# Value projection in units of one chunk, with both weight parts in one matmul and the halves added on DVE

## What is computed

```python
k = (cond @ wk.T + bk).reshape(B, L, H, D).transpose(0, 2, 1, 3)
v = (cond @ wv.T + bv).reshape(B, L, H, D).transpose(0, 2, 1, 3)
scores = jnp.einsum('bhnd,bhld->bhnl', q, k) * inv_sqrt_d + mask[:, None]
attn = jax.nn.softmax(scores, axis=-1)
o = jnp.einsum('bhnl,bhld->bhnd', attn, v)
```

## Time and profile before

| | |
|---|---|
| three runs | 997.35, 997.23, 993.93 us (median 997.23) |
| profiled execution | 993.16 us; span of its instructions 991.5 us |
| PE busy | 915.1 us, 92% of the span |
| PE's weight loads busy | 779.1 us, 79% |
| ACT busy | 565.5 us, 57% |
| DVE busy | 559.7 us, 56% |
| TensorE's granted clock, mean | 0.962 |

### The profile page before, as it was taken

One profiled execution on the slowest core, in us unless ns is written; L12 is line 12 of the kernel. 1 busy time (PEld: TensorE's weight loads), 2 busy tenths in 40 slices (PEclk: granted clock), 3 DMA queues, 4 the chain that ended last, 5 costly groups with the idle time before them and its releaser, 6 DMA issues. The chain is left out here.

```text
span 991.5 us, 21367 instructions
## 1 busy us (share of the span) xinstructions
PE 915.1 (92%) x7803; PEld 779.1 (79%) x7803; DVE 559.7 (56%) x1054; ACT 565.5 (57%) x976; POOL 74.5 (8%) x83
## 2 busy tenths in 40 slices
PE   5945989999999999999999999999999999979995
PEld 3534579898888888888888888888888888867773
DVE  2695465546565556565646564656555655563424
ACT  2513166766565656565756666666666666663442
POOL 0021000000000000000000000000000000063453
PEclk8965699999999999999999999999999999999998
DMA  6009657575656666656675666566656676420001
GB/s 177 7 34 258 155 130 166 130 161 143 149 146 146 155 137 151 146 151 135 157 150 145 138 157 147 152 136 160 146 153 137 158 149 141 98 46 2 2 0 38
DMA packets 67814, 126.19 MB, mean 127 GB/s; under 512 B 23568, under 2 KB 52408, under 8 KB 67512
## 3 DMA queue, kind: packets, MB, share of 16 engines
q1 hardware_dynamic: 66384, 124.66, 52.8%
q10 hardware_dynamic: 1344, 0.23, 0.2%
HBM read 46.30 MB, written 4.65 MB: 51 GB/s over the span
## 5 line engine op out<-in xcount | busy, mean ns | idle before, releaser
L1248 ACT ACTIVATE probsT<-ps_T 125x448 f32<-125x448 f32 x384 | 195.2, 544 | 182.1 <-PE ps_T L1122 182.1
L1349 DVE CUSTOM_DVE_ANT_0 scores<-ps_scores,mask_sb 112x1500 f32<-112x1500 f32 x128 | 220.0, 1719 | 17.4 <-PE ps_scores L1111 15.9
L1122 PEld LDWEIGHTS ps_T<-ident,scores 112*125 112x125 f32 x1536 | 198.7, 188 | 26.9 <-ACT probsT L1248 8.9
L1122 PE MATMUL ps_T<-ident,scores 112*125 112x112 f32 x1536 | 209.8, 273 | 6.4 <-issue 4.3
L1238 ACT ACTIVATE scores<-scores,shift 112x1500 f32<-112x1500 f32 x128 | 197.2, 1541 | 3.4 <-DVE shift L1349 3.0
L1091 PE MATMUL ps_proj<-room,wkvT 128*128 128x500 f32 x576 | 158.4, 411 | 6.0 <-DVE room L1332 3.3
L1099 PE MATMUL ps_proj<-wkvT,room 128*125 128x256 f32 x1152 | 159.8, 289 | 0.7 <-DVE v_sb L1327 0.6
L1136 PE MATMUL ps_out<-probsT,v_sb 125*32 125x112 f32 x3072 | 159.6, 260 | 0.0
L1136 PEld LDWEIGHTS ps_out<-probsT,v_sb 125*32 125x32 f32 x3072 | 144.2, 110 | 15.5 <-issue 10.6
L1099 PEld LDWEIGHTS ps_proj<-wkvT,room 128*125 128x125 f32 x1152 | 146.6, 189 | 10.4 <-issue 4.3
L1336 DVE SCALAR_TENSOR_TENSOR room<-ps_proj,xbk,room 128x500 fp32r<-128x500 f32 x96 | 70.8, 738 | 122.7 <-ACT room L1233 122.5
(11 more groups left out here) (252 smaller groups left out, 627.2 us busy)
## 6 DMA issues: line engine op xcount, KB each, us to landing
k_stack<-room SPq DMA_DIRECT2D x384, 187.5 KB, 3.9
ctx_rows<-in_ctx SPq DMA_DIRECT2D x48, 500.0 KB
mask_sb<-in_mask_BxSxS_ff SPq DMA_DIRECT2D x32, 328.1 KB
q_stack<-q_hi SPq DMA_DIRECT2D x32, 112.0 KB, 5.2
q_hi<-k_stack SPq DMA_DIRECT2D x4, 448.0 KB, 3.8
q_lo<-k_stack SPq DMA_DIRECT2D x4, 448.0 KB, 4.0
q_stack<-q_lo SPq DMA_DIRECT2D x16, 112.0 KB, 4.9
ctx_rows<-in_L_ffn_mask_idx SPq DMA_DIRECT2D x1, 1024.0 KB, 5.2
```

The lines of the kernel that those rows point to most:

```text
L1122: last = nc.tensor.transpose(ps_T[0:LT, (TB * t + k) % 2, j * PN:(j + 1) * PN], scores[:, t % 2, (k * TC + j) * LT:(k * TC + j + 1) * LT], ...
L1248: nc.scalar.activation(probsT[:, t % 2, k * TC:(k + 1) * TC], ps_T[0:LT, (TB * t + k) % 2, 0:TC * PN].rearrange("p (j n) -> p j n", j=TC), ...
L1349: nc.vector.tensor_tensor_reduce(out=split(scores[:, t % 2], NC), in0=ps_scores[0:PN, :, 0:LC], in1=split(mask_sb[:, a], NC), scale=-1.0, ...
```

## The change

A V unit is now one chunk, 12 units a batch in place of 6. The high part of the chunk is multiplied with both parts of the weights in one matmul of 512 columns, which gives the products in two halves of a bank; the low part times the high weights is added to the first half, in a matmul of 256 columns. DVE then adds the two halves while it moves them out, with a `tensor_reduce` over pairs of elements that lie 256 apart. The tables name the new units.

```diff
 UNITS = [
-    ([("X", 0, 0), ("X", 0, 1)], [("X", 1, 0), ("X", 1, 1)], [("X", 2, 0), ("V", 0, 0), ("X", 2, 1)]),
-    ([("K", 0, 0)], [("K", 0, 1)], [("K", 0, 2), ("V", 1, 0)]),
-    ([("V", 2, 0)], [("V", 3, 0)], [("V", 4, 0)]),
-    ([("K", 1, 0)], [("K", 1, 1)], [("K", 1, 2), ("V", 5, 0)]),
+    ([("X", 0, 0), ("X", 0, 1)], [("X", 1, 0), ("X", 1, 1)], [("X", 2, 0), ("V", 0, 0), ("X", 2, 1), ("V", 1, 0)]),
+    ([("K", 0, 0)], [("K", 0, 1)], [("K", 0, 2), ("V", 2, 0), ("V", 3, 0)]),
+    ([("V", 4, 0), ("V", 5, 0)], [("V", 6, 0), ("V", 7, 0)], [("V", 8, 0), ("V", 9, 0)]),
+    ([("K", 1, 0)], [("K", 1, 1)], [("K", 1, 2), ("V", 10, 0), ("V", 11, 0)]),
 ]
...
-         ("V", 0, 0), ("V", 1, 0), ("V", 2, 0), ("V", 3, 0), ("K", 1, 0), ("K", 1, 1), ("K", 1, 2), ("V", 4, 0), ("V", 5, 0)]
+         ("V", 0, 0), ("V", 1, 0), ("V", 2, 0), ("V", 3, 0), ("V", 4, 0), ("V", 5, 0), ("V", 6, 0), ("V", 7, 0),
+         ("K", 1, 0), ("K", 1, 1), ("K", 1, 2), ("V", 8, 0), ("V", 9, 0), ("V", 10, 0), ("V", 11, 0)]
...
-SCORES_AFTER = {12: 0, 14: 1}
+SCORES_AFTER = {16: 0, 18: 1}
...
-PREPARE_AT = {4: 1, 5: 2, 6: 3, 8: 4, 9: 5, 11: 6}
+PREPARE_AT = {4: 1, 5: 2, 6: 3, 8: 4, 10: 5, 14: 6}
...
-                        pe.wait_ge(unit_out, first + at[("X", (2 * p + 1) // TC, 1)] + 1 + 2)
-                        for j in range(2):
-                            c = slice((2 * p + j) * LT, (2 * p + j + 1) * LT)
-                            mm = [t for m in range(KT) for t in terms(cT_hi[:, m, c], cT_lo[:, m, c],
-                                                                      keep["wkvT"][:, 2, m], keep["wkvT"][:, 3, m])]
-                            for i, (w, x) in enumerate(mm):
-                                last = nc.tensor.matmul(ps_proj[0:LT, bank, j * D:(j + 1) * D], w, x, start=i == 0, stop=i == len(mm) - 1)
+                        pe.wait_ge(unit_out, first + at[("X", p // TC, 1)] + 1 + 2)
+                        c = slice(p * LT, (p + 1) * LT)
+                        both = ps_proj[0:LT, bank].rearrange("p (g d) -> p g d", g=2)
+                        for m in range(KT):
+                            x_hi, x_both = keep["wkvT"][:, 2, m], keep["wkvT"][:, 2:4, m]
+                            if m == 0:
+                                nc.tensor.matmul(both, cT_hi[:, m, c], x_both, start=True, stop=False)
+                            nc.tensor.matmul(ps_proj[0:LT, bank, 0:D], cT_lo[:, m, c], x_hi, start=False, stop=False)
+                        last = nc.tensor.matmul(both, cT_hi[:, m, c], x_both, start=False, stop=True)
...
-                        nc.vector.tensor_copy(v_sb[0:LT, a, 2 * p:2 * p + 2], split(ps_proj[0:LT, bank], 2)).then_inc(unit_out, 1)
+                        nc.vector.tensor_reduce(v_sb[0:LT, a, p], ps_proj[0:LT, bank].rearrange("p (g d) -> p d g", g=2), AX.X, ALU.add).then_inc(unit_out, 1)
```

## The result

Four runs of the changed kernel took 1060.28 to 1067.88 us, median **1064.4 us**, against 995.58 us for the kernel before beside it (four runs, 993.85 to 997.35). The ratio is **1.0699**, with a 95% interval of 1.0669 to 1.0728: 68.8 us more. The forecast was 1043 us, 48 us more. The profiled execution took 1066.7 us, its span is 1065.0 us, 73.5 us more than before.

A forecast was written before the change was run, and what follows sets the result against it. PE was taken to bound the kernel; plain batches 25.6, result batches 22.7, before the loop +1.0 and matmuls -1.1 summed to +48.2 us: 1041.4 from the profiled 993.2, or 1045 by the median, stated as 1043 us, range 1024 to 1066.

The forecast's parts named there:

- dear reduction: Rival A's case of a costlier DVE reduction; half of its price was counted in the range.
- 45 stalls: Places in the sum where PE waits, each given an error of 0.1 us in the range.
- Matmuls: V on PE: 12 matmuls become 8 per two chunks, wide ones 0.232 us each; 1.1 us saved in duo 2.
- rival B: Wide V matmuls on PE are cheap, 0.119 us each: 1011 us, still slower; chance 0.05.
- Reduction: DVE's reduction of each V chunk takes 0.69 us, like the copy; 66 us more DVE work.
- Rival A: DVE's reduction of V is dear, 1.21 us: 1073 us; chance 0.10.
- Plain batches: Second V unit waits for a drain: +1.02 us in duo 0, +1.09 in duos 1 and 3; 25.6 us over 8.
- Result batches: R starts later: +1.44 us in duo 0, +0.80 in duos 1 and 3, +0.2 in duo 2; 22.7 over 7.
- Rival C: PE only looks full, another chain sets the pace: time stays at 993 to 997 us; chance 0.05.
- Before the loop: Four V units after the last K unit: +1.0 us; eight earlier V units' 1.5 us covered by ACT's wait.
- twice a batch: In plain batches, the second V unit's wait for K's drain costs +1.09 us in duo 1 and again in duo 3.

The follow-up runs named there:

- E7: The kernel before with PE's loop of six rounds written out, nothing else: 990.09 us, ratio 0.9955.
- E5: The changed kernel with PE's loop of six rounds written out, other engines keeping theirs: 1036.71 us, ratio 1.0429.
- E1: The kernel before with one wait added, for K's drain ahead of V's second chunk in duo 3 of the loop's plain batches: 1021.92 us, ratio 1.0278.
- E9: E7 with V ahead of K in the last slots of duos 1 and 3, all batches: 989.28 us, ratio 0.9944.
- E11: E7 with V ahead of K in duos 1 and 3 of the result batches only: 988.98 us, ratio 0.9944.
- E10: The changed kernel with last slots of duos 0, 1 and 3 reordered, PE's loop written out, six narrow matmuls and a plain copy per chunk: 992.54 us, ratio 0.9974.
- E2: The changed kernel with duo 3's last slot in plain batches as V, K, V in place of K, V, V: 1048.85 us, ratio 1.0538.
- E4: The changed kernel with last slots of duos 1 and 3 as V, K, V (plain) and V, V, K, R (result batches): 1030.96 us, ratio 1.0368.

## Why the prediction was right, and where it fell short

Right: the direction, the mechanism, the durations, and that PE's waits count one for one. The time lay within the range, 2 us under its upper end, and 21 us above the forecast. That the range held is luck: 16 us of its upper half stood for a dear reduction, which did not come, and what came in its place was not in it. (Its 45 stalls are 52 by the sum's own places, with R in duo 2; that is 0.7 us.)

- *Matmuls.* A wide one starts 0.23 us ahead of the next matmul (206.69 to 206.92, and 208.96 to 209.19), as taken from 0.227 us for 500 columns. The 131 ns that the Trainium skill gives (TensorE: Matmul & The Clock Gate, section "Back-to-back issue gap") are not seen here; rival B falls.
- *Reduction.* 684 ns, for 0.69 taken. Rival A falls.
- *Plain batches.* Duo 1 +1.07 (1.09), duo 0 +1.04 (1.02), of which 0.13 is a second half of X that starts later behind the first, taken as unchanged, and the V unit behind it costs 0.1 less than said. *Result batches.* Duo 0 +1.44 (1.44), duo 2 +0.22 (0.2), duo 1 +0.80 (0.80): K starts at 256.44 and R at 260.42, 3.98 us, for 3.18 before. E7 and E5 check the sum of all: 46.6 us for 48.2.
- *Rival C*, that PE only looks full. It falls too: the stalls went into the time whole.

**Before the loop: +2.7 us between the two profiled executions, for 1.0.** From the last K unit to the first transposes, before and after:

```profile
126.13 1.64 PE L1091 MATMUL ps_proj<-room,wkvT 128*128 128x500 f32 x6 [2.17 <-DVE room L1336]
```

```profile
127.63 1.53 PE L1092 MATMUL ps_proj<-room,wkvT 128*128 128x500 f32 x6
...
133.49 1.03 PE L1125 MATMUL ps_T<-ident,scores 112*125 112x112 f32 x8
```

That is 4.70 us before (to 130.83) and 5.86 after: +1.16, about as said. But the K unit itself starts 1.5 us later: the 1.5 us of the eight V units ahead, which I took as covered by ACT's wait for a DMA, came through. The stretch ahead of it, after:

```profile
114.63 1.75 DVE L1435 TENSOR_TENSOR probsT<-ps_scores,probsT 8x1536 f32<-8x1536 f32 x1 [5.11 <-DMA probsT<-gate]
...
117.62 0.79 PE L1100 MATMUL ps_proj<-wkvT,room 128*125 128x512 f32 x1 [7.07 <-DVE v_sb L1330]
...
122.14 0.85 PE L1114 MATMUL ps_scores<-k_stack,q_stack 96*112 96x500 f32 x3
...
125.78 0.68 ACT L1236 ACTIVATE room<-ps_proj,xbk 128x500 fp32r<-128x500 f32 x1 [6.87 <-PE ps_proj L1092]
```

PE stood 7.07 us for a V unit's reduction. The reductions stood on DVE behind an instruction that waited 5.11 us for another DMA. PE came to the scores behind the V units at 122.14, 3.5 us later than before (118.59); ACT's wait at the key unit ended with PE, at 125.78, and no more with the DMA, at 124.63. The cover was gone. The price of that case stood in the text; its likelihood was misjudged.

Behind the wait the granted clock was 0.50 from 117.6 to 120.4 us, where the kernel before had 1.00 from 117.0 to 118.6: the first V unit took 1.45 us (117.62 to 119.07) and the second 1.28, for 0.7 each at the full clock, 1.3 us together. That the two banks now hold two chunks, and not four, is not shown to be the reason. E1, E9 and E11, with the old units, have such a wait too (7.6, 6.2 and 7.3 us). It is short (0.6 to 1.5 us) in the three traces whose granted clock was 0.50 from 100 to 110 us (before, E7, E10), and long in the ten others (clock 0.80 to 1.00). The first transposes start at 127.5 to 131.2 us in the five traces with units of two chunks, and at 130.1 to 133.5 in the eight with one, 2.3 us later in the mean. So how much of the 1.5 us comes from the change is open.

**The step that failed: "twice a batch" for +1.09.** Duo 3 of a plain batch was priced as duo 1. In five of its eight cases PE's branch follows. The profile had the sign of it, 4.3 us of "issue" at the transposes in five places, 0.81 us in the one shown above; I did not ask what the second V unit's wait would do there. Those holes and the clock behind them cost 27.7 us in place of 4.1: **23.6 us** (22.2 with each run against the kernel before beside it), as much as the whole miss of 21. Had I known that the first start lies some 4 us behind the last satisfied wait, which the five places of the trace before show (4.0 to 4.6 us) but which took the experiments to tell, the idle time alone could have been worked out: 0.8 us of work behind the wait leaves 3.2 us, five times, 16 us.

## What to carry to other kernels

A wait that is moved close to the end of a loop's body is not priced like the same wait elsewhere: find the last wait ahead of the branch, and see that some 4 us of issued work lie behind it, or write the rounds out on the engine that bounds. When units are made smaller over the same two banks, each drain has less work to hide behind; list, unit by unit, which drain lay under which matmuls before pricing what the smaller unit saves. And compare a stretch ahead of the steady batches over several executions before giving its difference a cause: with the same units, here it ended up to 3.7 us apart.

## What the runs showed of the hardware that was not expected

- From the last satisfied wait of PE ahead of its loop's branch to the first matmul of the next round it took 3.7 us (E2), 3.9 us (changed kernel), 4.1 us (before) and 4.6 us (E1) in the places shown, and 3.7 to 4.6 us over all 35 places of the seven traces, with 0.7 to 3.1 us of matmuls in between. Written out, the same place took 0.85 us (E5). What in that time is the branch and what the fetch of the next instructions no run tells.
- A hole of 2.9 us on PE was followed by 3.4 us at the lower level of the granted clock, and the eight transposes there took 1.92 us instead of 1.02. In the kernel before, holes of up to 1.3 us at the same place had no such stretch behind them. The length alone does not tell: in E4 holes of 2.43 and 2.45 us left the clock at 1.00 for the next 16 us, and holes of 2.41 and 2.48 us did not (0.89 as a mean over 16 us).
- A reduction over pairs of elements 256 apart, read from PSUM, took 684 ns for 512 elements, the same as a copy of 512 (688); a copy of 256 took 419 ns.
